# The prologue of a gated recurrence with a routed expert layer: the product of two weight matrices in 16-bit halves, and three moves around it

## The reference, cut to what matters

```python
xn = _layernorm(x, gamma, beta)
w = jax.nn.sigmoid(xn @ Wx @ Ww + bw)      # the decay
k = xn @ Wk
v = xn @ Wv
r = jax.nn.sigmoid(xn @ Wr)
state = (1.0 - wt)[..., None] * state + kt[..., None] * vt[..., None, :]
y = jnp.einsum('bhs,bhst->bht', rt, state)
return (y @ Wo, state_f)
```

## Time and profile before

| | us |
|---|---|
| median of 3 runs | 743.26 |
| lowest, highest | 740.24, 745.68 |
| profiled execution, its own time | 740.32 |
| its span, first to last instruction | 738.5 |
| PE, DVE, ACT, POOL busy | 709.7, 494.5, 378.0, 288.3 |
| mean granted TensorE clock | 0.991 of full speed |

### The profile page before, as it was taken

One profiled execution on the slowest core, in us unless ns is written; L12 is line 12 of the kernel. 1 busy time (PEld: TensorE's weight loads), 2 busy tenths in 40 slices (PEclk: granted clock), 3 DMA queues, 4 the chain that ended last, 5 costly groups with the idle time before them and its releaser, 6 DMA issues. The chain is left out here.

```text
span 738.5 us, 17426 instructions
## 1 busy us (share of the span) xinstructions
PE 709.7 (96%) x6205; PEld 516.4 (70%) x6205; DVE 494.5 (67%) x1087; ACT 378.0 (51%) x746; POOL 288.3 (39%) x254
## 2 busy tenths in 40 slices
PE   9999899999999999999999988999999999999994
PEld 4677777777878778777876876666666666666641
DVE  3857968869788687796978775544444444444487
ACT  3866754656557556676485632433333233432264
POOL 0574565464664545655522002333333333333110
PEclk9999999999999999999999999999999999999998
DMA  8824465254552554537410036465565555523955
GB/s 322 314 70 154 145 214 169 101 176 145 173 180 96 185 172 148 177 115 248 144 73 16 31 132 221 162 208 206 175 216 211 211 210 205 200 86 100 361 217 191
DMA packets 40139, 127.01 MB, mean 172 GB/s; under 512 B 4224, under 2 KB 4608, under 8 KB 38144
## 3 DMA queue, kind: packets, MB, share of 16 engines
q1 hardware_dynamic: 31024, 99.48, 38.5%
q0 software_dynamic: 6880, 22.55, 9.1%
q10 hardware_dynamic: 2160, 3.93, 1.5%
HBM read 81.12 MB, written 44.83 MB: 171 GB/s over the span
## 5 line engine op out<-in xcount | busy, mean ns | idle before, releaser
L1109 DVE COPY_PREDICATED ST<-msk,pS 128x256 f32<-128x256 uint8 x224 | 121.2, 570 | 52.5 <-issue 24.5
L766 POOL TENSOR_TENSOR piece_parts<-piece,piece_parts 128x1024 f16<-128x1024 f32 x48 | 104.0, 2168 | 96.0 <-ACT piece_parts L711 96.0
L1909 POOL DMA_INDIRECT y_scratch<-ysb,desti x43 | 42.6, 990 | 163.4 <-DVE ysb L1814 163.4
L1602 PE MATMUL pH<-ring,xgh 128*128 x344 | 103.0, 299 | 1.0 <-issue 0.6
L1603 PE MATMUL pH<-ring,xgh 128*128 x344 | 102.9, 299 | 0.0
L1604 PE MATMUL pH<-ring,xgl 128*128 x344 | 102.9, 299 | 0.0
L760 POOL TENSOR_TENSOR RL<-RL,AM 128x256 f32<-128x256 f32 x96 | 72.5, 755 | 71.1 <-ACT RL L703 64.8
L404 PE MATMUL pS<-RL 64*128 64x64 f32 (+2 forms) x1536 | 89.1, 265 | 0.0
L404 PEld LDWEIGHTS pS<-RL 64*128 64x128 f32 (+1 forms) x1536 | 84.4, 178 | 2.2
L1798 DVE TENSOR_TENSOR hid<-pH,sil 128x320 f32<-128x320 f32 x43 | 21.2, 492 | 95.8 <-ACT sil L1677 95.8
L744 DVE TENSOR_TENSOR RL<-RL,AM 128x256 f32<-128x256 f32 x96 | 70.5, 734 | 8.9 <-ACT RL L690 6.8
(11 more groups left out here) (253 smaller groups left out, 1539.4 us busy)
## 6 DMA issues: line engine op xcount, KB each, us to landing
piece<-in_w_experts SPq DMA_DIRECT2D x48, 512.0 KB, 4.8
w_split_scratch<-piece_parts SPq DMA_DIRECT2D x48, 512.0 KB, 3.8
ring<-w_split_scratch SPq DMA_DIRECT2D x12, 2048.0 KB
yin<-y_scratch SPq DMA_DIRECT2D x16, 512.0 KB, 11.8
out_x<-X SPq DMA_DIRECT2D x8, 512.0 KB, 2.8
x_scratch<-X ACTq DMA_DIRECT2D x15, 256.0 KB, 2.0
X<-in_x SPq DMA_DIRECT2D x2, 1536.0 KB, 17.8
RL<-in_wxT SPq DMA_DIRECT2D x4, 256.0 KB, 5.4
```

What stands on the lines that cost most here:

```text
L766: g.tensor_tensor(piece_parts[buf][:, 1, :], piece[buf][:, :], piece_parts[buf][:, 0, :], ALU.subtract).then_inc(piece_lo, 1)
L1109: v.copy_predicated(out[:, :, :, 0 if lv == 0 else 1, :], msk[:, lv, :, :].rearrange(shape, m=m), pS[:, :, lv * S:(lv + 1) * S].rearrange( ...
L1602: pe.matmul(p[:, 0, 0:F], xgh[par][:, k, :], wh, start=(k == 0), stop=False)
```

## The change

Four edits, all in the prologue.

1. Of Wx*Ww only slice `kt` = 0 stays in 32 bits. For slices 1 to 3 ACT casts the slice of Wx^T and of Ww to 16 bits (6 casts of 128x512, behind `normalise(0)`), DVE makes the low halves (6 subtractions), and PE makes three 16-bit matmuls where there was one in 32 bits. The halves lie in the tiles of Wo's and Wv's halves, which get their own content later.
2. PE turns x of pair 0 (jobs (0, 0) and (0, 1)) behind the first slice instead of the second.
3. DVE writes `low_x(0, 0)` ahead of `part_stats(1)` instead of behind it.
4. ACT takes the decay jobs (0, 2) and (0, 3) ahead of the first cast of Wo instead of behind it.

```diff
+        (wx_h, wx_l), (ww_h, ww_l) = (wo_h, wo_l), (wh["v"], wl["v"])
...
             for kt in range(KT):
-                pe.wait_ge(wz_in[kt], 32)
+                if kt == 0:
+                    pe.wait_ge(wz_in[kt], 32)
+                else:
+                    pe.wait_ge(wz_parts, 2 * kt)
                 for m in range(KT):
-                    i = pe.matmul(pS[:, m, :], wxT_sb[:, kt, m * P:(m + 1) * P], ww_sb[:, kt, :],
-                                  start=(kt == 0), stop=(kt == KT - 1))
+                    cols = slice(m * P, (m + 1) * P)
+                    if kt == 0:
+                        pe.matmul(pS[:, m, :], wxT_sb[:, kt, cols], ww_sb[:, kt, :], start=True, stop=False)
+                        continue
+                    pe.matmul(pS[:, m, :], wx_h[:, kt, cols], ww_h[:, kt, :], start=False, stop=False)
+                    pe.matmul(pS[:, m, :], wx_h[:, kt, cols], ww_l[:, kt, :], start=False, stop=False)
+                    i = pe.matmul(pS[:, m, :], wx_l[:, kt, cols], ww_h[:, kt, :], start=False, stop=(kt == KT - 1))
                     if kt == KT - 1:
                         i.then_inc(wz_full, 1)
-                if kt == 1:
+                if kt == 0:
                     pe.wait_ge(consts_in, 32)
                     job(0, 0, 0)
                     job(0, 1, 0)
...
             normalise(0)
+            for kt in range(1, KT):
+                a.wait_ge(wz_in[kt], 32)
+                a.copy(wx_h[:, kt, :], wxT_sb[:, kt, :]).then_inc(wz_halves, 1)
+                a.copy(ww_h[:, kt, :], ww_sb[:, kt, :]).then_inc(wz_halves, 1)
             high(0)
...
             high_x(1, 1)
+            take(0, 2, 0)
+            take(0, 3, 0)
             a.wait_ge(w_in[5], 32)
             a.copy(wo_h[:, 0:2, :], wo_stage[0]).then_inc(wo_hi, 1)
-            take(0, 2, 0)
-            take(0, 3, 0)
...
             part_terms(0)
+            for kt in range(1, KT):
+                v.wait_ge(wz_halves, 2 * kt - 1)
+                v.tensor_tensor(wx_l[:, kt, :], wxT_sb[:, kt, :], wx_h[:, kt, :], ALU.subtract).then_inc(wz_parts, 1)
+                v.wait_ge(wz_halves, 2 * kt)
+                v.tensor_tensor(ww_l[:, kt, :], ww_sb[:, kt, :], ww_h[:, kt, :], ALU.subtract).then_inc(wz_parts, 1)
...
+            low_x(0, 0)
             part_stats(1)
-            low_x(0, 0)
             part_terms(1)
```

More of the change, by code:

```diff
@@ L213, in attention @@
         setup_done = sem("setup_done")
+        wz_halves = sem("wz_halves")
+        wz_parts = sem("wz_parts")
         wz_full = sem("wz_full")
```

## The result

The changed kernel takes 747.61 us in the median (742.51 to 750.60, 20 runs), the kernel before 743.40 us (740.24 to 746.40, 20 runs). The ratio is 1.0053, 95% interval 1.0036 to 1.0071: slower by about 3.9 us (the two medians lie 4.2 us apart), and clear of noise. The profiled execution has a span of 746.0 us, 7.5 us more than that of before; the medians say that about half of this repeats.

What follows compares the result with a forecast made beforehand. It took PE, busy 96% of the span, as the bound, with ACT the chain from 21.81 to 31.84. Terms -2.3 + 2.3 + 1.9 + 1.6 = +3.5 us took the median from 743.26 to 746.8, range 741.5 to 750.0.

Steps and rivals of the forecast that it cites:

- The product, -2.3 us on PE: Prologue product of Wx and Ww on PE: 36 16-bit matmuls replace 12, ending at 20.8 against 23.07, -2.3 us.
- Casts and subtractions at nothing: ACT's six casts and DVE's six subtractions for the product fit into idle time: 0 us, bounds 0 and +1.0.
- low_x ahead of the statistics, +1.0 us on ACT, and the product's gain lost: Pair 1 in the prologue: `normalise(1)` starts 1.0 us later on ACT, so the product's whole 2.3 us is lost.
- POOL behind the cast of Wo, +1.9 us: Prologue: POOL's `low_out(0)` waits for the later cast of Wo and delays the key levels, +1.9 us, bounds 1.6 and 2.6.
- The clock, +1.6 us: Behind PE's new hole from 26.0 to 30.2, one half-clock stretch over jobs (0, 2) and (0, 3), +1.6 us.
- The lock between DVE and GpSimd, 0.4 us more: DVE's second decay product stands behind `low_out(0)`, POOL's first key level maybe behind that product: some 0.4 us, not counted.
- The sum, +3.5 us: Whole kernel: product -2.3, lost gain +2.3, POOL +1.9, clock +1.6 give +3.5 us, median 746.8.

Runs made afterwards that it cites:

- e3: Changed kernel with its third edit undone, so the statistics of pair 1 run ahead of low_x on DVE; ratio 1.0036 to the kernel before.
- e6: Changed kernel with third and fourth edits undone, keeping only the product in halves and the turns behind the first slice; ratio 1.0019 to the kernel before.
- e1: Changed kernel with POOL's first low half of Wo moved behind the key levels of chunk 0; ratio 1.0037 to the kernel before.
- e4: Changed kernel with its fourth edit undone, so the first cast of Wo is ahead of the decay takes again; ratio 1.0039 to the kernel before.
- e5: Kernel before with the fourth edit alone, decay takes ahead of the first cast of Wo; ratio 1.0020 to the kernel before.
- e2: Changed kernel with 3 and 6 discarded matmuls in PE's two waits, in front of the turns of pair 1; ratio 1.0035 to the kernel before.
- e8: Changed kernel with DVE's low half of y of chunk 0 ahead of the decay products of pair 1; ratio 1.0051 to the kernel before.
- e7: Changed kernel with the third edit undone and the first cast of Wo between the two decay takes; ratio 1.0013 to the kernel before.
- e9: Kernel before with as many more instructions as the changed kernel has (tiny matmuls, copies, fills) and no other change; ratio 1.0016 to the kernel before.
- e10: Kernel before traced once more, unchanged; scores 39.08 us behind ACT's cast of Wk, wait at the read of the state 1.66 us.
- e11: Changed kernel traced once more, unchanged; scores 41.81 us behind ACT's cast of Wk, wait at the read of the state 4.16 us.
- e12: Kernel before with DVE's low half of y of chunk 0 ahead of the decay products of pair 1; 741.44 us against 742.69, ratio 0.9979.

## Why the prediction was right, point by point

- **The product, -2.3 us on PE.** Right: 36 matmuls at 0.22 us, and from its start to its end 12.1 us (9.12 to 21.2) against 14.8 (8.30 to 23.07). Counted from the cast of Wk it ends 2.3 us sooner. It ended ahead of what could use it.
- **Casts and subtractions at nothing.** Right. The casts ended ahead of Wk's load, for which ACT still waited 0.55 us, and the subtractions ahead of Wk's low half.
- **low_x ahead of the statistics, +1.0 us on ACT, and the product's gain lost.** Right: 8.42 instead of 7.42 us from the cast of Wk to `normalise(1)`, and e3 gives it back. Job (0, 2) started at 30.57, with 0.47 of later loads: 0.1 us later than before. Without this edit and the fourth, e6 gets 1.0 of the 2.3 us.
- **POOL behind the cast of Wo, +1.9 us.** The mechanism was right, by e1, e4 and e5. From the second decay take to the scores it is 19.36 us, against 17.3 before and 16.90 in e4: 2.1 to 2.5 us. Counted from the cast of Wk, the take itself is 0.5 us sooner than before once the 1.5 us of the clock are taken off. Together that is 1.7 us at the scores (40.62 in e2 and 40.66 in e5, both with the clock up at the takes, against 38.92). The prediction's own terms, 2.6 less 0.5, give 2.1 and not the 1.9 that it carried "with rounding"; the size was right all the same.
- **The clock, +1.6 us.** 1.5 us in the changed kernel's trace, 0.9 to 1.7 us over all four traces where it fell. It fell in four of the five traces with these waits (the changed kernel twice, e4, e8) and not in e1, so an average execution pays less than the full term; how much less is not shown.
- **The lock between DVE and GpSimd, 0.4 us more.** On record from the Trainium skill, SBUF — State Buffer, "Who interferes with whom", and left out of the sum. Its first half came: a decay product of DVE (128x128, the third), begun at 39.66 beside POOL's 2.16 us, took 2.10 us and ended at 41.76, where it took 0.71 us in e1. Its second half did not: POOL's first key level started at once, at 41.57, and took 0.88 us, as against 0.86 us in e1 and 0.84 in e4. DVE was held by POOL, POOL hardly by DVE, and the 0.4 us did not arise. The pair of rows that the prediction read for it had a third party: before, POOL's key level of 1.19 us started at 36.96, while DVE's low half of x ran until 37.45 (e7 has the same meeting, with 1.90 us).
- **The sum, +3.5 us.** The prologue came to 3.1 and 2.7 us in the two traces, and the median to 3.9 us. Much of this agreement is luck. The sum holds only terms of the prologue, and says that "PE, and the engines that it feeds, are all late by the same" behind it. That step did not hold. e1 has a prologue as short as that of the kernel before and is 2.7 us slower in the median, clear of noise (its trace loses 0.4 us at chunk 1 and 1.4 near 300 to 325 us); from the changed kernel to e1 3.0 us go from the prologue and 1.2 us from the median. So what was added behind the prologue is about as large as any term of the sum, and the prediction has no term for it. Shown in traces are 1.4 us near 300 to 325 us that come with added instructions (e9), and 1.2 to 3.1 us at chunk 1 where POOL's subtraction starts ahead of DVE's last small product (e10 and e11). How these add up in a median stays open: e8 takes the wait at chunk 1 out of the changed kernel, and its ratio stays at 1.0051.

## What to carry to other kernels

A faster product on the busiest engine gave 1.0 of its 2.3 us at most (e6), because the engine that takes its results was nearly full, and nothing once another edit put 1.0 us on that engine; look for the stretch in which the consumer has no wait, and count from there. When an instruction is moved on one engine, look on the other engines for what waits for it and stands ahead of something urgent: here one cast that moved by about 5 us held unmoved work on POOL, and the scores behind it, for about 2 us. And an edit of the first 30 us can change how loads meet the compute 250 us later; a median, and not the shift at the end of the edited part, says what it is worth.

## What the runs showed of the hardware that was not expected

A product of 128x8 on DVE, 0.17 us in the trace of before, took twelve times as long where a subtraction of POOL began 0.02 us ahead of it. DVE, then POOL, of the changed kernel in chunk 1:

```profile
82.05 2.13 DVE L737 TENSOR_TENSOR dec_end<-AM 128x8 f32<-128x8 f32 x1
84.22 0.69 DVE L1243 TENSOR_TENSOR yTl<-pY,yTh 128x512 f16<-128x512 f32 x1
```

```profile
82.03 2.13 POOL L777 TENSOR_TENSOR piece_parts<-piece,piece_parts 128x1024 f16<-128x1024 f32 x1 [2.05 <-ACT piece_parts L722]
```

The same before:

```profile
78.42 0.17 DVE L726 TENSOR_TENSOR dec_end<-AM 128x8 f32<-128x8 f32 x1
78.62 0.69 DVE L1228 TENSOR_TENSOR yTl<-pY,yTh 128x512 f16<-128x512 f32 x1
```

```profile
78.46 2.12 POOL L766 TENSOR_TENSOR piece_parts<-piece,piece_parts 128x1024 f16<-128x1024 f32 x1 [2.10 <-ACT piece_parts L711]
```

Here the product started 0.04 us ahead of POOL's subtraction. PE waits for the low half of y behind it, so 0.06 us of order decide over 2 us of PE: the read of the state waited 1.66 us before and 3.68 us in the changed kernel. The low half itself, which reads one of its inputs from PSUM, took 0.69 us although it lay within POOL's subtraction. The Trainium skill (SBUF — State Buffer, "Who interferes with whom") says that a DVE instruction with two SBUF inputs contends with a GpSimd instruction that reads SBUF, for a port pair that is an exclusive lock. The trace agrees: the small product, with both inputs in SBUF, ends with POOL's whole instruction.

Nor was it expected that the same waits of PE, 0.73 and 1.63 us in e1 and 0.67 and 1.63 us in the changed kernel, are followed by a fall of the clock in one execution and not in the other (1.00 against 0.66 over 30 to 35 us), nor that in e12 the clock stays at 1.00 over a stretch in which PE is busy for 2.18 of 5 us.
